# First layer's attention output turned by VectorE instead of TensorE, and the input's statistics and the value masks moved to ScalarE

## The reference

```python
def L0(x, emb, src_mask, ...):                 # softmax attention over 256 keys
    xn = layer_norm(x, norm_w, norm_b)
    q = (xn @ q_w + q_b).reshape(B, T, H, -1); k = (xn @ k_w + k_b).reshape(B, T, H, -1)
    att = jnp.einsum('bnhl,bmhl->bnmh', q, k) + (1.0 - mask) * -1000000.0
    att = jax.nn.softmax(att, axis=2)
    v = ((xn @ v_w + v_b) * src_mask[:, :, None]).reshape(B, T, H, -1)
    y = jnp.einsum('bnmh,bmhl->bnhl', att, v).reshape(B, T, D)
    scale, shift = jnp.split(jax.nn.silu(emb) @ emb_w + emb_b, 2)
    h = layer_norm(y, sb_norm_w, sb_norm_b) * (1.0 + scale) + shift
    return x + jax.nn.silu(h) @ out_w + out_b

def L1(x, emb, src_mask, ...):                 # linear attention: softmax of q over features, of k over tokens
    ...
    return x + jax.nn.silu(h) @ film_out_W + film_out_b
```

## Time and profile before

| what | us |
|---|---|
| median of 3 runs (867.24 to 867.9) | 867.61 |
| the profiled execution | 869.6 |
| its span, first to last instruction | 867.8 |
| TensorE busy in the span | 832.3 |
| VectorE busy | 773.2 |
| ScalarE busy | 679.0 |
| GpSimd busy | 679.9 |

### The profile page before, as it was taken

One profiled execution on the slowest core, in us unless ns is written; L12 is line 12 of the kernel. 1 busy time (PEld: TensorE's weight loads), 2 busy tenths in 40 slices (PEclk: granted clock), 3 DMA queues, 4 the chain that ended last, 5 costly groups with the idle time before them and its releaser, 6 DMA issues.

```text
span 867.8 us, 23658 instructions
## 1 busy us (share of the span) xinstructions
PE 832.3 (96%) x8092; PEld 686.9 (79%) x8092; DVE 773.2 (89%) x1590; ACT 679.0 (78%) x1208; POOL 679.9 (78%) x1165
## 2 busy tenths in 40 slices
PE   4999999999999999999999988999999999999996
PEld 4777777777777777777777656899999999999996
DVE  6689999999998999999998967899999999999976
ACT  2247777777777777777778796899999999999975
POOL 3375878878888888888786337899999999999965
PEclk9899999999999999999999999999999999999999
DMA  8854665565656565655654424345454444444311
GB/s 258 263 175 165 198 219 187 207 209 191 220 183 212 179 222 181 221 196 196 219 178 164 142 64 107 96 126 144 152 149 143 136 142 140 138 150 141 116 31 62
DMA packets 129847, 143.69 MB, mean 166 GB/s; under 512 B 13312, under 2 KB 85984, under 8 KB 129600
## 3 DMA queue, kind: packets, MB, share of 16 engines
q1 hardware_dynamic: 129728, 142.19, 50.5%
HBM read 49.50 MB, written 38.11 MB: 101 GB/s over the span
## 4 chain that ended last, share of the span: by engine, by line
PE 77%; DVE 13%; issue 6%; POOL 1%; ACT 1%; SPq 1%; DMA 0%; DVEq 0%; ACTq 0%; POOLq 0%
PE psY L1721 12%; PE psX L1600 11%; PE psT L1600 10%; PE psM L1600 10%; DVE sb_cm L1158 6%; PE psT L1700 5%; PE psY L1600 5%; PE psT L1679 4%; PE psT L1883 3%; PE psY L1836 3%; PE psT L1611 3%; PE psM L1700 3%; PE psY L1746 2%; DVE sb_xF L1172 2%; PE psM L1679 2%
## 5 line engine op out<-in xcount | busy, mean ns | idle before, releaser
L1158 DVE TENSOR_REDUCE sb_cm<-psT 128x4 f32<-128x1024 f32 x168 | 202.8, 1213 | 20.5 <-PE psT L1700 20.3
L741 ACT ACTIVATE sb_P<-psT 128x1024 f32<-128x1024 f32 x176 | 177.8, 1026 | 42.6 <-PE psY L1721 23.5
L1721 PE MATMUL psY<-sb_P,sb_Vp 128*17 128x256 f32 x2048 | 129.4, 381 | 1.9 <-DVE sb_yr L1193 1.2
L1158 DVE TENSOR_REDUCE sb_cm<-psM 128x4 f32<-128x1024 f32 x88 | 106.7, 1213 | 11.5 <-PE psM L1700 11.5
L741 ACT ACTIVATE sb_P<-psM 128x1024 f32<-128x1024 f32 x80 | 82.0, 1025 | 21.6 <-PE psY L1721 11.7
L1600 PE MATMUL psX<-sb_xT,sb_W0h 128*128 128x256 f32 x488 | 93.6, 294 | 0.0
L1721 PEld LDWEIGHTS psY<-sb_P,sb_Vp 128*17 128x17 f32 x2048 | 50.3, 97 | 46.8 <-DVE sb_yr L1193 1.9
L521 POOL TENSOR_TENSOR sb_qp<-sb_qp 128x512 fp32r<-128x512 f32 x64 | 82.3, 1285 | 5.3
L1700 PE MATMUL psT<-sb_Ks,sb_Qs 64*128 64x256 f32 x672 | 76.6, 310 | 2.6 <-DVE sb_cm L1158 2.5
L1679 PE MATMUL psT<-sb_Qs,sb_Ks 64*128 64x256 f32 x704 | 75.5, 298 | 1.6 <-ACT sb_P L741 1.4
L1600 PEld LDWEIGHTS psX<-sb_xT,sb_W0h 128*128 128x128 f32 x488 | 71.4, 192 | 4.6 <-ACT sb_qp L764 0.2
(11 more groups left out here) (215 smaller groups left out, 2553.4 us busy)
## 6 DMA issues: line engine op xcount, KB each, us to landing
sb_Qs<-sb_qp SPq DMA_DIRECT2D x96, 256.0 KB
sb_Ks<-sb_qp SPq DMA_DIRECT2D x96, 256.0 KB
sb_xt<-in_x SPq DMA_DIRECT2D x32, 256.0 KB, 3.4
y_normed<-sb_Yn SPq DMA_DIRECT2D x32, 256.0 KB, 2.7
sb_u<-y_normed SPq DMA_DIRECT2D x128, 64.0 KB, 2.6
out<-sb_v SPq DMA_DIRECT2D x31, 256.0 KB, 2.4
x_biased<-sb_xo SPq DMA_DIRECT2D x28, 256.0 KB, 2.3
sb_u<-x_biased SPq DMA_DIRECT2D x28, 256.0 KB, 3.3
```

The source lines that it names most:

```text
L741: a.activation(P[G % 4][:, :], pairs[place["S", n, g][0]][:, :], ACT.Exp).then_inc(s_ex, 1)
L1158: v.tensor_reduce(cm[n % 2][:, 4 * j:4 * j + 4], scores, AX.X, ALU.max, negate=True).then_inc(s_mx, 1)
L1721: ins = pe.matmul(psY[32 * j:32 * j + 17, y0:y0 + T], Vp[n % RING][:, m, 4 * gr + j, :], Pj[:, c0:c0 + 256], start=(m == 0), stop=(m == 1))
```

## The change

- **y.** For sequences 0 to 27 (`TAIL = B - 4`) VectorE turns `psY` itself with two stream transposes (32x32 blocks) straight from PSUM (`yblock`), 128x512 each. They go in stripes of four tokens: a block takes every fourth column. The reciprocal of the sums is taken per filling (`yroot`), GpSimd multiplies (`share`), four moves by SP from tile to tile (`ymove`) bring the heads together, and VectorE takes the statistics when they have landed (`ylanded`). The eviction by ScalarE and the transposes by TensorE are left out for these. The last four sequences keep the way of before. `ynorm` and `ystore` come one turn later.
- **x.** `nblocks` moves the blocks straight from `xs` to `xB`; `x_normed` is gone. `xturn` writes every fourth element.
- **Statistics of x** from sequence 10 (`SUMMED`): ScalarE sums x (`xsum`), GpSimd makes the mean (`xmean`), ScalarE sums the squares of the differences (`xsquares`), GpSimd makes the root in `xnorm`.
- **Masks of v** by ScalarE (`vmask`).
- The lists of GpSimd and SP are in another order, and the order of heads in q's and k's weights and in the value matmuls is another one.

```diff
+TAIL = B - 4
+SUMMED = BY_BLOCK + 4
...
+        blocked, moved = (t[:, :, :].rearrange("p q t -> p (q t)") for t in yT)
+        yG = [blocked[:, 512 * i:512 * i + 512].rearrange("p (g b c) -> p g b c", g=2, b=8) for i in range(2)]
+        yq = moved[:, 0:512]
+        yrs = [yr[:, :, :], moved[:, 512:1024].rearrange("p (k d) -> p k d", k=2)]
...
-            def nstore(n):
+            def nblocks(n):
+
                 sp.wait_ge(s_xn, n + 1)
-                sp.dma_start(xnd[n], xs[:, :, :, :, :].rearrange("p a i k c -> p (a i k c)")).then_inc(s_nd, 16)
-
-            def nblocks(n):
-
-                sp.wait_ge(s_nd, 16 * (n - BY_BLOCK + 1))
                 if n > BY_BLOCK:
                     sp.wait_ge(s_xf, n - BY_BLOCK)
...
+                tile = xB[:, :, :].rearrange("p k t -> p (k t)")
+                for a in range(4):
+                    sp.dma_start(tile[32 * a:32 * a + 32, :], xs[:, a, :, :, :].rearrange("p i k c -> p (i k c)"))\
+                        .then_inc(s_nb, 16)
 
...
+            def ymove(n):
+
+                sp.wait_ge(s_yq, 2 * n + 2)
+                if n >= 2:
+                    sp.wait_ge(s_y, n - 1)
+                for j in range(4):
+                    sp.dma_start(yrs[n % 2][:, :, 64 * j:64 * j + 64], yq[32 * j:32 * j + 32, :]).then_inc(s_yl[n % 2], 16)
 
...
+                if 0 <= t - 5 < TAIL:
+                    ymove(t - 5)
+                if t >= BY_BLOCK and ok(t + 2):
+                    nblocks(t + 2)
+                if 0 <= t - 6 < TAIL:
+                    ystore(t - 6)
+                if TAIL <= t - 5 < B:
                     ystore(t - 5)
+                if t >= BY_BLOCK and ok(t + 2):
+                    xstore(t + 2)
+                if t >= BY_BLOCK and ok(t + 4):
+                    xload(t + 4)
...
-                if ok(t + 2) and t + 2 > BY_BLOCK:
-                    nstore(t + 2)
...
+            def xmean(n):
+                g.wait_ge(s_sx, 2 * (n - SUMMED) + 2)
+                g.wait_ge(s_xn, n)
+                g.tensor_scalar(nm[:, 0:2], sx[:, 0, :], -1.0 / D, 0.0, ALU.mult, ALU.add).then_inc(s_rs, 1)
+
             def xnorm(n):
...
+                else:
+                    g.wait_ge(s_sq, 2 * (n - SUMMED) + 2)
+                    g.tensor_scalar(ve[:, k], sx[:, 1, :], 1.0 / D, EPS, ALU.mult, ALU.add).then_inc(s_rs, 1)
+                    g.wait_ge(s_rs, 3 * n + 2)
+                    g.tensor_tensor(rs[:, k], ve[:, k], ph[:, :], ALU.pow).then_inc(s_rs, 1)
...
+            def share(n, half):
+
+                g.wait_ge(s_yi, 2 * n + half + 1)
+                if half == 0 and n >= 1:
+                    g.wait_ge(s_yl[(n - 1) % 2], landed(n - 1, 2, 4))
+                root = ri[:, half, :].rearrange("p (g b a) -> p g b a", g=2, a=1).to_broadcast([128, 2, 8, DH])
+                g.tensor_tensor(yq.rearrange("p (b g d) -> p g b d", b=8, g=4)[:, 2 * half:2 * half + 2],
+                                yG[half][:, :, :, 0:DH], root, ALU.mult).then_inc(s_yq, 1)
+
...
-            def vmask(n):
...
             for t in range(B):
                 if t >= BY_BLOCK:
                     xlow(t)
-                if BIASED <= t + 1 < B:
+                if ok(t - 5):
+                    share(t - 5, 1)
+                if t >= BY_BLOCK and ok(t + 2):
+                    xnorm(t + 2)
+                if BIASED <= t + 1 <= BY_BLOCK:
                     xbias(t + 1)
-                for_later(t)
-                if ok(t - 5):
-                    ynorm(t - 5)
+                if ok(t - 6):
+                    ynorm(t - 6)
+                if ok(t - 4):
+                    share(t - 4, 0)
+                if SUMMED <= t + 3 < B:
+                    xmean(t + 3)
                 if ok(t - 2):
                     csplit(t - 2)
-                if ok(t - 1):
-                    vmask(t - 1)
                 if t + 1 < BY_BLOCK:
                     xnorm(t + 1)
+                elif t + 1 == BY_BLOCK:
+                    xnorm(t + 2)
                 elif ok(t + 2):
-                    xnorm(t + 2)
+                    xbias(t + 2)
+                for_later(t)
                 if ok(t):
                     split(t, 0)
                     split(t, 1)
+                if t + 1 == BY_BLOCK:
+                    xbias(t + 2)
+            share(B - 5, 1)
+            ynorm(B - 6)
+            csplit(B - 2)
             ynorm(B - 5)
-            csplit(B - 2)
-            vmask(B - 1)
...
+            def xsum(n):
+
+                a.wait_ge(s_x[n % 2], landed(n, 2))
+                a.wait_ge(s_xtr, BY_BLOCK)
+                if n > SUMMED:
+                    a.wait_ge(s_rs, 3 * n - 2)
+                    a.wait_ge(s_sq, 2 * (n - SUMMED))
+                for k in range(2):
+                    a.activation(xn[:, k, :], xt[n % 2][:, k, :], ACT.Identity, accum_out=sx[:, 0, k:k + 1])\
+                        .then_inc(s_sx, 1)
+
+            def xsquares(n):
+
+                a.wait_ge(s_rs, 3 * n + 1)
+                a.wait_ge(s_sx, 2 * (n - SUMMED) + 2)
+                for k in range(2):
+                    a.activation(xn[:, k, :], xt[n % 2][:, k, :], ACT.Square, bias=nm[:, k:k + 1],
+                                 accum_out=sx[:, 1, k:k + 1]).then_inc(s_sq, 1)
+
+            def vmask(n):
+                a.wait_ge(s_vb, n + 1)
+                if n >= RING:
+                    a.wait_ge(s_pv, 4 * (n - RING) + 4)
+                for k in range(2):
+                    ins = a.activation(Vp[n % RING][:, k, :, 0:16], vb[:, k, :].rearrange("p (h d) -> p h d", d=DH),
+                                       ACT.Identity, scale=mT[:, k, n:n + 1])
+                ins.then_inc(s_v, 1)
+
...
                 exps(t, 0)
-                if ok(t - 4):
-                    yturn(t - 4, 0)
+                if ok(t - 1):
+                    vmask(t - 1)
                 exps(t, 1)
+                if SUMMED <= t + 3 < B:
+                    xsum(t + 3)
                 exps(t, 2)
                 exps(t, 3)
                 if ok(t):
...
                 exps(t, 4)
-                if ok(t - 4):
-                    yturn(t - 4, 1)
-                if ok(t - 2):
-                    cturned(t - 2)
                 exps(t, 5)
                 if ok(t):
                     qk(t, 1)
                 exps(t, 6)
+                if ok(t - 2):
+                    cturned(t - 2)
                 exps(t, 7)
+                if SUMMED <= t + 3 < B:
+                    xsquares(t + 3)
...
-                v.transpose(xF[:, :, :].rearrange("p i t -> p (i t)").rearrange("p (q b s) -> p b q s", q=4, b=4),
+                v.transpose(xF[:, :, :].rearrange("p i t -> p (i t)").rearrange("p (q s b) -> p b q s", q=4, b=4),
...
+            def yblock(n, half):
+
+                v.wait_ge(s_pv, 4 * n + 2 * half + 2)
+                if n >= 1:
+                    v.wait_ge(s_yq, 2 * n - 1 + half)
+                v.transpose(yG[half].rearrange("p g (b k) c -> p g k b c", k=2),
+                            psY[:, :].rearrange("p (g k s b) -> p g k b s", g=2, k=2, b=4)).then_inc(s_yg, 1)
+
+            def yroot(n, half):
+                v.wait_ge(s_yg, 2 * n + half + 1)
+                v.reciprocal(ri[:, half, :], yG[half].rearrange("p g b c -> p (g b) c")[:, :, 16]).then_inc(s_yi, 1)
+
+            def ylanded(n, k):
+
+                v.wait_ge(s_yl[n % 2], landed(n, 2, 4))
+                if n >= 1:
+                    v.wait_ge(s_y, n)
+                v.bn_stats(st[:, 2 + k, :], yrs[n % 2][:, k, :]).then_inc(s_ys, 1)
+                v.wait_ge(s_ys, 4 * n + 2 * k + 1)
+                v.bn_aggr(mv[:, 2 + k, :], st[:, 2 + k, :]).then_inc(s_ys, 1)
+
...
+                if ok(t - 4):
+                    yblock(t - 4, 0)
                 maxima(t, 2)
+                if t > BY_BLOCK and ok(t + 1):
+                    xturn(t + 1)
+                if ok(t - 4):
+                    yroot(t - 4, 0)
                 if 1 <= t < BY_BLOCK - 1:
                     stats(t + 1, 0)
-                elif t >= BY_BLOCK - 1 and ok(t + 2):
+                elif t == BY_BLOCK - 1:
                     stats(t + 2, 0)
-                if ok(t - 5):
-                    ystats(t - 5, 1)
                 maxima(t, 3)
                 maxima(t, 4)
...
+                if ok(t - 4):
+                    yblock(t - 4, 1)
                 maxima(t, 5)
-                if t + 1 >= BY_BLOCK and ok(t + 1):
+                if BY_BLOCK - 1 <= t <= BY_BLOCK:
                     xturn(t + 1)
+                if ok(t - 4):
+                    yroot(t - 4, 1)
                 maxima(t, 6)
-                if ok(t - 4):
-                    divide(t - 4, 0)
                 maxima(t, 7)
-                if ok(t - 4):
-                    ystats(t - 4, 0)
-                if t >= BY_BLOCK:
-                    divide(t - 4, 1)
+                if ok(t - 5):
+                    ylanded(t - 5, 0)
+                    ylanded(t - 5, 1)
                 if ok(t):
```

(29 more changed lines are left out.)

153 lines of the change are left out of this document (75 added, 78 removed).

## The result

The changed kernel is slower: 881.74 us median of 4 executions (872.94 to 883.79) against 867.52 for the kernel before on the same chip, a ratio of 1.0144 with a 95% interval of 1.0075 to 1.0213. The forecast's sum was 848.1, with 836 to 862. The executions of the changed kernel spread over 11 us, those of before over 0.7. The profiled one took 882.53, its span is 880.7.

A forecast was written before the change was run, and what follows sets the result against it. TensorE, busy 14.80 of 14.93 us a turn, was taken as the bound; three near-equal loops would then set turns of 14.14 instead of 14.95. Gain 19.5 from 869.6 profiled gives 850.1, median 848.1 us; range 836 to 862.

The forecast's parts named there:

- loop C: Chain of waits through SP's queue, the landing of y's moves and GpSimd, back to the store: 11.45 us + L.
- L: Time for the fourth move of y to land after its issue starts; taken as 2.2 to 2.6 us.
- the rival with the opposite sign: Slower: moves of y land late, loop C with L above 3.5 us; 885 us at L = 4.2; chance 0.11.
- loops A and B: Chains of waits bounding a turn: A through ScalarE's exponents, 14.10 us; B through VectorE's maxima and transposes, 14.09 us.
- some 1.0 gained: Turns 4 to 6, where VectorE keeps the statistics of x: their gain put at 1.0 us.
- loop A: Chain through ScalarE's exponents, masks and sum of x, TensorE's S4 and ScalarE's bias of k: 14.10 us a turn.
- 14.14 and 13.75: Forecast turn, 0.04 us over loop A, and the turn TensorE alone could reach, in us.
- the two groups: TensorE's two groups of transposes of y, which the change removes: 0.63 + 0.55 = 1.2 us a turn gained.
- my bounds: Extra time of a VectorE transpose that jumps four elements: taken as 0, with 0.25 and 0.53 us kept.
- The passage: Switch to the old path for the last four sequences, after the changed turns: a loss of 0.5 us.
- The second layer: The part after the loop of 32 turns, which the diff touches only in one wait.

The follow-up runs named there:

- e2: Changed kernel with GpSimd's first product of y moved behind the mean, the split of the maxima and the bias of x; 865.3 us, ratio 0.997.
- e14: e2 plus masks and sum of x later, sequence 7's blocks turned early, TensorE's shifts transpose back before k; 859.3 us, ratio 0.990.
- e15: Kernel before with only the x part: blocks straight from tile to tile, transpose of x writing every fourth element; 876.1 us, ratio 1.009.
- e4: Changed kernel with the statistics of x kept on VectorE for all sequences; 876.8 us, ratio 1.011.
- e8: e2 and e4 together: late product, and statistics of x by VectorE; 864.5 us, ratio 0.995.
- e16: Changed kernel with masks and sum of x later on ScalarE, GpSimd's mean between its splits, product of y still early; 875.5 us, ratio 1.010.
- e9: e2 with the four moves of y issued by ScalarE's queue behind exponent 3 instead of by SP; 905.8 us, ratio 1.043.
- e6: e2 with the normalised x moved in one transfer instead of four, so the result is not the reference's; 860.4 us, ratio 0.989.
- e17: e14 with x and y in one transfer each, so the result is not the reference's; 854.5 us, ratio 0.983.
- e13: Changed kernel, product still early, with x in one transfer instead of four, so the result is not the reference's; 872.7 us, ratio 1.004.

## Why the prediction was wrong

The step of it that failed is loop C, "GpSimd waits for that landing before the first product", which I took as 11.45 + L and 13.65 to 14.05, below the other loops. It measured 15.18 as the mean of 18 turns and 14.41 at the least, so it was the longest loop in every one of them. The mechanism, a loop that closes through the landing and the store of x, was in the prediction as the rival with the opposite sign, at 0.11. That rival wanted L above 3.5 us, though, and L had a mean of 2.70: most of the excess came from a term that I had not let vary, the issues. Three things were off.

*Its terms.* From the store of x to the fourth move I had 8.72 us: it is 9.91 as a mean, and 9.45 and 10.18 in the two turns shown. Of the 0.73 that was missing in the quiet one, 0.53 lie in the moves. They start 0.69 apart (0.65 and a short gap) instead of 0.51, because I took them from loads out of HBM. The rest up to the mean comes from issues that are slow now and then: 10 of the 270 in these stretches take more than 1 us, and up to 2.2. SP waits for something in them for 0.06 us a turn only. GpSimd's part is 2.54 and not 2.73. The landing of 2.43 was in my range, that of 3.73 not.

*The middle of a loop that varies.* I took quiet values for the terms and compared the sum with loops A and B. But the issues and the landing come anew in each turn, and a slow one lengthens the turn in full: the bias of x and the split of the maxima stand behind the wait, and SP's store starts as soon as the bias is done. Of what I missed in turns 8 to 31, 344.8 - 325.3 = 19.5 us, the late product takes back 12.2 (332.6 in e2). The same wait costs more where the changed order begins: 7.8 us once in turn 5, and from turn 4 to turn 8 e2 takes 6.3 us less. My "some 1.0 gained" in turns 4 to 6 was wrong by sign: they lost 4.2 us, and 8.8 were lost from turn 4 to turn 8.

*The floor below.* The remaining 7.3 us are loop A and TensorE. With C out of the way the step is 14.48, and 14.20 without the masks between the exponents, against my 14.14 and 13.75. Loop A I had led through ScalarE's bias of k (7.47 us from S4 to the values); the longer way is TensorE's own, 7.80 us almost without a gap (e2, timeline of TensorE, S4 and values):

```profile
391.78 0.51 PE L1793 MATMUL psM<-sb_Qs,sb_Ks 64*128 64x256 f32 x4
...
399.58 1.92 PE L1834 MATMUL psY<-sb_P,sb_Vp 128*17 128x256 f32 x32
```

And TensorE gave 14.95 - 14.04 = 0.91 and not 1.2: the two groups' matmuls up to their successors in the trace of before, 0.53 + 0.41. The 0.33 of idle didn't add to that, and the transpose of the shifts between S6 and S7 cost 0.16 until e14 moved it back.

By the other points of the prediction:

- **VectorE's new work.** Right for y: 0.710 us, no extra for a reading that jumps four elements in PSUM. Wrong for x: 1.106 us against 0.702, an extra of 0.40, inside my bounds, where I had taken 0. The Trainium skill (SBUF — State Buffer, section on door 1) says that SBUF has lines of 16 bytes and each crossing pays; the trace agrees for the writing in SBUF. It gives PSUM lines of 8 bytes and says that a pattern which isn't contiguous there slows matmuls; for a VectorE transpose that reads PSUM so, the trace shows no slowing. In the change the 0.40 is covered; the x part on the kernel before is 0.3 us a step slower (e15), where the transpose stands on the longest chain with 0.4 us a turn more. No run separates it from the direct moves.
- **ScalarE.** The pairs are 0.80 (masks), 0.79 (sums) and 0.99 (squares) by their successors in e2, against 0.78, 0.84 and 1.02: right, and not the cause (e4, e8, e16).
- **The queue.** I counted 11.5 us of issues a turn: 13.4 us are issued (some 255 in 19 turns).
- **Landing.** 2.3 us as a median with pieces of 256 bytes (L366, up to 4.0), 2.2 with pieces of 512 (L349, up to 3.6). The prediction took two sentences from the Trainium skill (DMA: Bandwidth & Descriptors), line rate from 512 bytes in the specifications and no penalty from SBUF to SBUF in the section on small descriptors; the medians agree with the second. The late landings, which cost more, are in neither.
- **The passage** lost 2.2 instead of 0.5. **The second layer** took 3.0 us more, forecast 0. In the other traces of this study it takes 0.6 to 5 us more than in the one trace of before, so much of it may be scatter; no run was made to find out why, and it stays open.

## What to carry to other kernels

A transfer whose landing gates an engine's in-order list sets a loop of issues, landing and all that stands ahead of the next issue: put the consumer that waits as late in the list as its own readers allow; here that one line gave 16.5 us. Where such a loop comes within a microsecond of the longest one, count it by the mean with its late cases, take each issue from a transfer of the same kind, and don't compare a quiet value. And a unit taken from a full TensorE gives the distance to its successor, not its length plus the idle time beside it.

## What the runs showed of the hardware

- A transfer between two SBUF tiles holds the issuing queue for 0.60 us (128 partitions to 32, pieces of 512 bytes) and 0.65 (32 to 128, pieces of 256 bytes), where 64 KB out of HBM took 0.45 as a median and 0.50 as a mean (before, L342); single issues take up to 2.2. On ScalarE's queue a move takes 0.65 as well, and the engine gets no new work meanwhile (e9). The Trainium skill (DMA: Bandwidth & Descriptors, anatomy of one DMA) has some 50 ns for the dispatch and calls the generation of descriptors small, for the path through GpSimd's queue. No transfer here takes that path; on SP's queue the shortest issues take 0.32 us.
- A VectorE transpose of 128x512 costs 0.40 us more if it writes every fourth fp32 element in SBUF, and nothing more if it reads so in PSUM.
- In the changed kernel and most of its versions TensorE's weight loads stand for 0.6 to 2.4 us in some of the turns 5 to 31 with nothing named that they wait for (five times in the changed kernel, 3.9 us). In these turns the kernel before has none of 0.6 us or more, nor have e15 (x direct alone), e6 (x in one transfer) and, with 6 issues and some 1,300 pieces fewer a turn, e17.
- With three transfers fewer a turn the same 15 issues of SP's queue took 8.84 instead of 9.15 us (e13 against the changed kernel) and 8.71 instead of 9.21 (e6 against e2), as a mean of 18 turns.
